# Second experts' output rows scattered to token order in the block loop, and summed from plain loads

## The reference

```python
x = x + _L0_gnn_ref(_layernorm(x, axis=-1), L0_gnn_W, src, dst, edge_weight)
x = x + _L0_ffn_ref(_layernorm(x, axis=-1)[None], ...)[0]      # attention, then 64 experts, top 2, capacity C
x = x + _L1_gnn_ref(_layernorm(x, axis=-1), edge_index, ...)
x = x + _L1_ffn_ref(_layernorm(x, axis=-1)[None], ...)[0]      # 8 experts, top 2
...
# _L0_ffn_ref: y = einsum('efh', gelu(buf @ w1 + b1)) + b2;  ys = y[ef, posc] * (gf * keep)[:, None]; sum over the 2 choices
# _L1_ffn_ref:
top_vals, top_idx = jax.lax.top_k(logits, TOP_K)
top_w = jax.nn.softmax(top_vals, axis=-1)
for e in range(E):
    hdn = jax.nn.gelu(flat @ W1[e] + b1[e], approximate=False)
    y = hdn @ W2[e] + b2[e]
    out = out + gates[:, e:e + 1] * y
```

## Time and profile before

| | us |
|---|---|
| median of three runs | 1457.34 |
| the profiled execution | 1460.3 |
| its span, first to last instruction | 1458.5 |
| first_experts, about | 775 to 1040 |
| second_convolution, about | 1040 to 1239 |
| second_router, about | 1239 to 1294 |
| second_experts, about | 1294 to 1408.7 |
| finish | 1408.7 to 1458.5 |

### The profile page before, as it was taken

One profiled execution on the slowest core, in us unless ns is written; L12 is line 12 of the kernel. 1 busy time (PEld: TensorE's weight loads), 2 busy tenths in 40 slices (PEclk: granted clock), 3 DMA queues, 4 the chain that ended last, 5 costly groups with the idle time before them and its releaser, 6 DMA issues. The chain is left out here.

```text
span 1458.5 us, 24082 instructions
## 1 busy us (share of the span) xinstructions
PE 1388.2 (95%) x7949; PEld 899.5 (62%) x7950; DVE 757.1 (52%) x1604; ACT 464.2 (32%) x1153; POOL 255.7 (18%) x336
## 2 busy tenths in 40 slices
PE   8999999999999999999998999999789999989958
PEld 3688854455467777777455777776345555646632
DVE  7999956562168788887563333332440013543411
ACT  3599940021055555555121111111430021211111
POOL 1133310000000000000213555554000000012233
PEclk9999999999999999999999999999999999699988
DMA  6000000020050000000535999996600000913335
GB/s 156 30 0 0 0 0 0 0 87 0 0 170 2 2 2 1 2 2 2 162 71 173 327 314 319 320 315 208 145 1 0 0 0 0 324 46 111 113 96 167
DMA packets 93109, 133.79 MB, mean 92 GB/s; under 512 B 14459, under 2 KB 51729, under 8 KB 92911
## 3 DMA queue, kind: packets, MB, share of 16 engines
q1 hardware_dynamic: 74553, 107.76, 23.7%
q0 software_dynamic: 14592, 18.19, 4.4%
q10 hardware_dynamic: 3894, 6.89, 1.3%
HBM read 115.09 MB, written 31.41 MB: 100 GB/s over the span
## 5 line engine op out<-in xcount | busy, mean ns | idle before, releaser
L1301 PEld LDWEIGHTS ps<-b_r 128*128 128x128 f32 x1024 | 124.4, 192 | 35.0 <-issue 33.5
L1301 PE MATMUL ps<-b_r 128*128 128x78 f32 x1024 | 122.2, 272 | 1.9 <-DVE b_r L1378 1.3
L1310 PE MATMUL ps<-b_r 128*78 128x512 f32 x256 | 122.0, 600 | 0.0
L590 PE MATMUL ps<-b_r 125*125 125x160 f32 x660 | 118.4, 315 | 0.0
L505 ACT ACTIVATE b_r<-b_r 125x125 f32<-125x125 f32 x330 | 107.6, 389 | 9.2 <-DVE b_r L400 4.8
L1175 POOL TENSOR_TENSOR b_x<-b_x,b_r 125x512 f32<-125x512 f32 x10 | 12.7, 1268 | 534.1 <-DVE b_r L1118 534.1
L939 PEld LDWEIGHTS ps<-b_r 125*64 125x64 f32 x1600 | 85.3, 136 | 24.6 <-issue 22.8
L1361 ACT ACTIVATE b_r<-ps,b_r 128x78 f32<-128x78 f32 x128 | 34.7, 323 | 203.9 <-PE ps L1301 188.0
L902 PE MATMUL ps<-b_r 64*125 64x417 f32 (+1 forms) x480 | 95.3, 529 | 1.4 <-DVE ps L1031 1.2
L939 PE MATMUL ps<-b_r 125*64 125x125 f32 x1600 | 94.7, 272 | 1.3 <-ACT b_r L967 1.3
L119 PE MATMUL ps<-b_ones_bf 125*128 125x512 bf16 x322 | 80.1, 409 | 13.5 <-PEq L1233 5.2
(11 more groups left out here) (272 smaller groups left out, 2250.2 us busy)
## 6 DMA issues: line engine op xcount, KB each, us to landing
b_r<-L_ffn_w SPq DMA_DIRECT2D x128, 512.0 KB
b_r<-L_ffn_W SPq DMA_DIRECT2D x2, 4096.0 KB, 20.5
y<-b_r ACTq DMA_DIRECT2D x24, 256.0 KB, 2.4
y<-b_x SPq DMA_DIRECT2D x2, 2400.0 KB
rows<-b_r SPq DMA_DIRECT2D x2, 2400.0 KB
b_r<-y SPq DMA_DIRECT2D x10, 480.0 KB
b_x<-x SPq DMA_DIRECT2D x5, 480.0 KB
out<-b_x SPq DMA_DIRECT2D x10, 240.0 KB
```

Source lines behind the costliest of these rows:

```text
L590: last = pe.matmul(T.ps[:P, 2 + b, 0:WC], T.weighted[:, b, j, :], T.cells[:, b, j, :], start=(j == 0), stop=(j == CJ - 1))
L1301: last = pe.matmul(T.ps[:, 2 + r % 2, f * CAP:(f + 1) * CAP], T.ew1[r % WS][:, k, f * 128:(f + 1) * 128], T.ex_t[:, r % 2, k, :], start=(k ...
L1310: last = pe.matmul(T.ps[:CAP, 4 + r % 2, :], T.eh[:, r % 2, f, :], T.ew2[r % WS][:, f, :], start=(f == 0), stop=(f == FK - 1))
```

## The change

- **second_experts scatters.** ScalarE's stores (L1764) are gone. POOL scatters the output rows of block b-4 behind the gather of block b, with an indirect DMA to y1, which is now in token order for each choice. For that it copies a column of places (T.sids) into T.ey_ids before each scatter. Input and output rows have four slots instead of two, and the loop's body has four steps instead of two.
- **The sums move into second_experts.** `finish` is gone. When the last four scatters have landed, SP issues ten plain loads of y1, one for each pair of tiles and each choice. TensorE multiplies gates and biases behind its last block (as first_experts does), VectorE adds these ten products to x, and then adds gate times row for both choices with two instructions for each tile. ScalarE issues the stores of the output, for pairs of tiles, each as 120 and 5 partitions.
- **Rows by partition first.** y0 and y1 hold PLACES = 1280 rows for each choice, and the row of token t*125 + p is p*10 + t instead of t*125 + p. So a load of two tiles for one choice reads 4 KB in a row for each of 128 partitions; 20 loads (L1258) become 10.
- **Router work.** T.row_i is no longer computed in either router (three instructions on VectorE in the first, two in the second). The places (T.sids) are computed by three linked instructions at the start of first_experts and of second_experts instead of in the router. The second router gains the ten matmuls of `make_choices`.
- **Fills.** y0 is filled in projections (from T.feats) instead of in attention, with the spare rows of y1.

```diff
-
-def choice_ids(dve, T, bank, rows, columns):
-
-    return dve.scalar_tensor_tensor(out=T.sids[:rows, 0:columns], in0=T.ps[:rows, bank, 0:columns],
-                                    scalar=float(N), in1=T.ids_low[:rows, 0:columns], op0=ALU.mult, op1=ALU.add)
+
+def choice_ids(dve, link, T, bank, choice_bank, rows, columns):
+
+    place, low = T.place_ids[:rows, 0:columns], T.ps[:rows, bank, 0:columns]
+    link(dve.tensor_scalar(place, low, float(NT), float(NOWHERE), ALU.mult, ALU.add))
+    link(dve.tensor_tensor(place, T.ps[:rows, bank, columns:2 * columns], place, ALU.add))
+    return dve.scalar_tensor_tensor(out=T.sids[:rows, 0:columns], in0=T.ps[:rows, choice_bank, 0:columns],
+                                    scalar=float(PLACES), in1=place, op0=ALU.mult, op1=ALU.add)

...
-            spare = NB - 4 * FOURS
-            sp.dma_start(A.y1[4 * FOURS:NB].rearrange("b r d -> r b d"),
-                         T.feats.rearrange("p k n -> p (k n)")[:, 0:spare * D].rearrange("p (b d) -> p b d", b=spare))\
-              .then_inc(S.rows_filled, 16)
-            sp.wait_ge(S.rows_filled, 16)
+            feats = T.feats.rearrange("p k n -> p (k n)")
+            for j in range(TOP):
+                spare = A.y1[j * PLACES + NT * P:(j + 1) * PLACES].rearrange("(p t) d -> p (t d)", t=NT)
+                for c0, c1 in ((0, KD * N), (KD * N, NT * D)):
+                    sp.dma_start(spare[:, c0:c1], feats[0:128 - P, 0:c1 - c0]).then_inc(S.rows_filled, 16)
+            for j in range(TOP):
+                filled = A.y0[j * PLACES:(j + 1) * PLACES].rearrange("(p t) d -> p (t d)", t=NT)
+                for c0, c1 in ((0, KD * N), (KD * N, NT * D)):
+                    sp.dma_start(filled[:, c0:c1], feats[:, 0:c1 - c0]).then_inc(S.rows_filled, 16)
+            sp.wait_ge(S.rows_filled, 128)
...
-            for j in range(TOP):
-                for p0, p1 in ((0, 120), (120, P)):
-                    sp.dma_start(A.y0[j * N:(j + 1) * N].rearrange("(t p) d -> p t d", t=NT)[p0:p1], T.x[p0:p1])\
-                      .then_inc(S.rows_filled, 16)
-            sp.wait_ge(S.rows_filled, 80)
-
...
+            keep = T.keep
             link(dve.tensor_scalar(keep[:], T.position[:], float(CAP), None, ALU.is_lt))
             link(dve.tensor_tensor(T.gate[:], T.gate[:], keep[:], ALU.mult))
-
-            link(dve.tensor_scalar(row[:], T.position[:], float(CAP - 1), None, ALU.min))
-            link(dve.scalar_tensor_tensor(out=row[:], in0=T.expert[:], scalar=float(CAP), in1=row[:],
-                                          op0=ALU.mult, op1=ALU.add))
-            dve.tensor_copy(T.row_i[:], row[:])
             gate_rows(dve, link, T, E0, S.gates_ready)
             dve.wait_ge(S.table_made, 1)
             token_ids(dve, link, T, 7, CAP, E0)
-            dve.wait_ge(S.table_made, 2)
-            choice_ids(dve, T, 1, CAP, E0)

...
                 sp.wait_ge(S.ey_stored[slot], 16 * E0 // SLOTS)
             for i in range(NT // 2):
-                for p0, p1 in ((0, 120), (120, P)):
-                    for j, rows in enumerate((T.rows_a, T.rows_c)):
-                        sp.dma_start(rows[p0:p1, 2 * i:2 * i + 2],
-                                     A.y0[j * N:(j + 1) * N].rearrange("(t p) d -> p t d", t=NT)[p0:p1, 2 * i:2 * i + 2])\
-                          .then_inc(S.y_gathered[i], 16)
+                for j, rows in enumerate((T.all_a, T.all_c)):
+                    sp.dma_start(rows[:, 2 * i:2 * i + 2],
+                                 A.y0[j * PLACES:(j + 1) * PLACES].rearrange("(p t) d -> p t d", t=NT)[:, 2 * i:2 * i + 2])\
+                      .then_inc(S.y_gathered[i], 16)
...

+            link = Chain(dve, S.dve_chain, T.dve_at)
+            link(choice_ids(dve, link, T, 7, 1, CAP, E0))
             turned(0, 0)
...
             pe.wait_ge(S.placed, 3)
             make_table(pe, T, 7, BR, NB).then_inc(S.table_made, 1)
+            make_choices(pe, T, 3, BR, T.place, NB).then_inc(S.table_made, 1)
             pe.wait_ge(S.gates_ready, 2)
...

-            link(dve.scalar_tensor_tensor(out=row[:], in0=within[:], scalar=float(BR), in1=row[:], op0=ALU.mult, op1=ALU.add))
-            dve.tensor_copy(T.row_i[:], row[:])
             gate_rows(dve, link, T, E1, S.gates_ready)
...
-            gather_rows(pool, T, A.rows1, T.rx, BR, loops, S.rx_ids_ready, S.rx_turned, S.rx_loaded)
+            def token_column(q, r):
+                pool.tensor_copy(T.ex_ids[:, r % 4:r % 4 + 1], T.ids[:, bass.ds(q * 4 + r, 1)]).then_inc(S.rx_ids_ready, 1)
+
+            def place_column(q, r, c):
+                pool.tensor_copy(T.ey_ids[:, c:c + 1], T.sids[:, bass.ds(q * 4 + r, 1)]).then_inc(S.rx_ids_ready, 1)
+
+            def gather(q, r):
+                pool.indirect_dma_start(T.rx[:, r % 4, :], None, A.rows1,
+                                        bass.IndirectOffsetOnAxis(ap=T.ex_ids[:, r % 4:r % 4 + 1], axis=0),
+                                        bounds_check=N - 1, oob_is_err=False).then_inc(S.rx_loaded[r % 4], 16)
+
+            def scatter(q, r, stored):
+
+                if r + 1 < 8:
+                    wait_count(pool, S.ry_stored[(r + 1) % 4], q, 16, 16 * ((r + 1) // 4))
+                pool.wait_ge(S.ry_copied, q * 4 + (r + 1))
+                place_column(q, r + 1, (r + 1) % 4 if r + 1 < 8 else 4)
+                pool.indirect_dma_start(A.y1, bass.IndirectOffsetOnAxis(ap=T.ey_ids[:, r % 4:r % 4 + 1], axis=0),
+                                        T.ry[:, r % 4, :], None, bounds_check=TOP * PLACES - 1, oob_is_err=False)\
+                    .then_inc(stored, 16)
+
+            def turn(q, r):
+                wait_count(pool, S.rx_turned, q, 4, r - 2)
+                pool.wait_ge(S.rx_ids_ready, q * 8 + (r + 2 if r < 4 else 2 * r - 2))
+                token_column(q, r + 1)
+                gather(q, r)
+                if not isinstance(q, int) or r >= 4:
+                    scatter(q, r - 4, S.ry_stored[r % 4])
+
+            pool.wait_ge(S.places_ready, 1)
+            token_column(0, 0)
+            place_column(0, 0, 0)
+            loops = loops_of(pool)
+            for r in range(4):
+                turn(0, r)
+            with pool.Fori(0, loops) as q:
+                for r in range(4, 8):
+                    turn(q, r)
+            for r in range(4, 8):
+                turn(loops, r)
+            for r in range(8, 12):
+                pool.wait_ge(S.rx_ids_ready, loops * 8 + (r + 6))
+                scatter(loops, r - 4, S.ry_last)
+
+        @block.sync
+        def _(sp):
+            sp.wait_ge(S.ry_last, 64)
+            for i in range(NT // 2):
+                for j, rows in enumerate((T.all_a, T.all_d)):
+                    sp.dma_start(rows[:, 2 * i:2 * i + 2],
+                                 A.y1[j * PLACES:(j + 1) * PLACES].rearrange("(p t) d -> p t d", t=NT)[:, 2 * i:2 * i + 2])\
+                      .then_inc(S.y_gathered[i], 16)
...
+            pe.wait_ge(S.b2_loaded, 32)
+            for t in range(NT):
+                if t >= 2:
+                    pe.wait_ge(S.bias_added, NT + t - 1)
+                pe.matmul(T.ps[:P, t % 2, :], T.gates_t1[:, t * P:(t + 1) * P], T.b2_rows1, start=True, stop=True)\
+                  .then_inc(S.bias_done, 1)
...
-            def store(q, r, stored):
-                wait_count(act, S.ry_copied, q, 2, r + 1)
-                act.dma_start(A.y1[bass.ds(q * 2 + r, 1)].rearrange("o c d -> (o c) d"), T.ry[:, r % 2, :])\
-                   .then_inc(stored, 16)

             def step(q, r, last=False):
                 if not is_first(q, r):
                     turned(q, r - 1)
                 hidden(q, r)
-                if not is_first(q, r):
-                    store(q, r - 1, S.ry_last if last else S.ry_stored[(r - 1) % 2])

             act.preload_act_table(ACT.Gelu)
             end = blocks(act, step)
             turned(*end)
-            store(*end, S.ry_last)
-            act.wait_ge(S.ry_last, 32)
+
+            out = A.out.rearrange("(t p) d -> p t d", t=NT)
+            for i in range(NT // 2):
+                act.wait_ge(S.out_ready, 2 * i + 2)
+                for p0, p1 in ((0, 120), (120, P)):
+                    act.dma_start(out[p0:p1, 2 * i:2 * i + 2], T.x[p0:p1, 2 * i:2 * i + 2]).then_inc(S.out_stored, 16)
+            act.wait_ge(S.out_stored, 16 * NT)
...
+            link = Chain(dve, S.dve_chain, T.dve_at)
+            dve.memset(T.sids[:, NB:], 0)
+            choice_ids(dve, link, T, 7, 3, BR, NB).then_inc(S.places_ready, 1)
             dve.wait_ge(S.b11_loaded, 16)
             turned(0, 0)
             end = blocks(dve, step)
             output(*end)

...
             for t in range(NT):
...
+                dve.wait_ge(S.bias_done, NT + t + 1)
+                dve.tensor_tensor(T.x[:, t, :], T.ps[:P, t % 2, :], T.x[:, t, :], ALU.add).then_inc(S.bias_added, 1)
+            dve.wait_ge(S.bias_added, 2 * NT)
+            rows = (T.rows_a, T.rows_d)
             for t in range(NT):
```

(9 more changed lines are left out.)

154 lines of the change are left out of this document (49 added, 105 removed).

## The result

The changed kernel takes 1432.96 us (median of 4 runs, 1429.46 to 1435.79); the kernel before, on the same chip, 1455.62 (4 runs, 1453.16 to 1459.32). The ratio is 0.984 with a 95% interval of 0.981 to 0.988: 23 us, 1.6%, faster. The forecast was 1427 in a range of 1418 to 1441. The profiled execution, with which the terms are compared, has a span of 1429.8 us against 1458.5.

What follows compares the result with a forecast made beforehand. It took TensorE to bound the block loop, with 52.3 us behind it computing no expert. Gains 6.0 + 0.6 + 23.7 = 30.3 us, taken off the median 1457.34, gave 1427 us; range 1418 to 1441.

Steps and rivals of the forecast that it cites:

- The seam: Between first_experts and second_convolution: ten loads end before VectorE, TensorE idles less, fillers run fast; gain 6.0 us.
- The routers: First router: VectorE loses three linked instructions ahead of the gate rows, gain 0.6 us; second router: zero.
- Start of second_experts: POOL's first gather waits for four VectorE instructions and a second column copy; loss 0.3 us, bounds 0 and 1.2.
- The block loop: second_experts: POOL's step stays under 4.20 us, TensorE keeps 4.20; without ScalarE's store the last step gains 1.1 us.
- The tail: Behind the block loop: scatter, loads, sums, store end at 1434.8 against 1458.5 us; gain 23.7, loop's 1.1 and start's 0.3 included.
- the term of the bias products: Behind the block loop: ten bias products take 9.2 us, only just hidden by the first loads' arrival.
- The landing: Behind the block loop: y1's first pair of tiles, 1.05 MB, is in 5.3 us after SP's first issue.
- (a): Rival: loads stay at 207 GB/s, so the kernel's end comes 10.8 us later; time 1438 us; chance 0.13.
- (b): Rival: POOL sets the block loop's pace at 4.8 us a step, costing 11 us; time 1438; chance 0.12.
- (c): Rival: VectorE's instructions stop POOL's descriptor work, block-loop step 5.9 us, slower than before; time 1465; chance 0.05.
- (d): Rival: no gain between first_experts and second_convolution, SP's issues stay long or something else holds the barrier; 1433 us; chance 0.11.
- (e): Rival: the end behind the block loop is no shorter, scattered rows land late or sums wait; 1457 us; chance 0.03.

Runs made afterwards that it cites:

- seam_120: Changed kernel with y0 loaded by 20 transfers in 4 KB pieces, split into partitions 0 to 119 and 120 to 127; ratio 0.981 to the kernel before.
- early_expert: Changed kernel with TensorE reading the expert number before the two transposes, not between them and the hidden product; 1427.15 us, ratio 0.977 to the kernel before.
- gather_later: Changed kernel with POOL's gather of block r also waiting for TensorE's transposes of block r-3's hidden rows; 1432.03 us, ratio 0.980 to the kernel before.
- bias_early: Changed kernel with six of second_experts' ten bias products made at its start in place of 24 fillers; 1434.38 us, ratio 0.983 to the kernel before.
- tail_120: Changed kernel with y1 loaded by 20 transfers, split into partitions 0 to 119 and 120 to 127; 1438.99 us, ratio 0.986 to the kernel before.
- dve_copies: Changed kernel with one more VectorE copy, 128x512 float32 from SBUF to SBUF, in each block-loop step; 1432.62 us, ratio 0.982 to the kernel before.

## Why the prediction was right, and where it wasn't

The mechanism was right: the 52.3 us behind the last output copy were the place, and the seam the second. Of the 30.3 us forecast, 25.0 came from these places in the profiled executions (6.5 seam, -2.3 loop, 20.8 tail); 3.7 more lie between them, where the clock differs. The 25 agree with the 23 of the medians. That the profiled span, 1429.8, comes so near to the forecast 1428.2 is therefore luck: 3.7 us that nobody forecast stand in for most of what loop and tail fell short of.

- *The seam*: 6.0 forecast, 6.46 measured (21.55 - 15.09). Its steps held: SP done before VectorE, a short idle time, fast fillers. The reason given for SP's long issues, the slow rate alone, was incomplete: seam_120 has the slow rate and 7.5 us of issues.
- *The routers*: 0.6 forecast. TensorE's fillers of first_experts do start 1.1 us earlier (774.01 instead of 775.14), but the first scatter comes at the same time, with a longer clock dip in between (granted clock 0.50 from 784 to 788 us, 0.73 before). In the thirteen kernels with the changed kernel's code there it comes at 787.7 to 792.7 us, 791.15 before, so 0.6 us can't be told.
- *Start of second_experts*: 0.3 loss forecast, none measured: from the first filler to the first hidden product 7.17 us, 7.16 before.
- *The block loop*: this step failed. "TensorE keeps 4.20 a step" counted POOL's work and TensorE's data, but not the register load in TensorE's queue, on which the scatter's transfer now falls: 4.395 us, 3.6 us in all. The rows showed no idle time on TensorE, and yet 0.1 us of each 4.20 was a wait for that load. The 1.1 us at the last step was right: from the last hidden product to the last output copy it is 7.2 us, 8.5 before. early_expert and gather_later show both halves.
- *The tail*: 22.9 forecast, 20.8 measured. Mis-sized is the term of the bias products: 9.2 us, taken from 64-row products in the earlier trace rows, for products over 8 rows, which took 12.8. It was to be hidden by the landing and became what is waited for. The landing itself, 5.3 us for the first pair of tiles, came true (5.25 in bias_early) by luck: the 5.34 us of the earlier trace rows are the time of one gather of 125 rows, 0.26 MB, not of the 1.05 MB that the prediction puts there. The others: from the last copy to SP's first issue 3.3 (forecast 3.9), 20 sums 14.6 (15.8), the last store 4.0 (3.6), rate 405 to 422 GB/s (385).
- *The rivals*: (a) had the right condition, the split. Its price of 10.8 us is three times the 3 us of tail_120, but mostly because the bias products, which ran slow, cover the first loads; with fast ones it would be 8.7 by the estimate above. (b) is out: POOL's step is 3.2 us of 4.4, and both gaps, 0.57 and 0.16, are in it. (c) is out for this kernel by scatters of 0.98 to 1.03 us and by dve_copies. (d) and (e) are out by the rows; the time of (e), 1457, should have been 1451, since a tail that is no shorter leaves the 6.6 us of seam and routers.

## What to carry to other kernels

Where a transfer or a wait moves, look also at what it now runs beside in each step: register loads in an engine's queue don't count as busy, and a step can lose 0.2 us to one of them while every engine seems to have room. Take the length of a product from rows of the same shape, the rows in use included, since TensorE's clock may hang on them. Here the issues of a load grew with its pieces (5.0 to 10.2 us, 7.5 to 16.2 with the split), and its rate hung on its partitions: 128 partitions and long runs gave both. Before a small price is taken from an experiment, look at what else covers the wait in it.
